# The first aggregation behind two gates begun early, two tiles turned by products, and 14 repeated products in a wait

## The chip, the cores and the metric

The kernel runs on one core of a Trainium2 chip. The metric is the device time of one execution in microseconds (us). TensorE does the matrix products (the trace calls it PE, and its weight loads PEld), VectorE is DVE, ScalarE is ACT, GpSimd is POOL, and SyncE (SP) issues most transfers.

## The reference

256 nodes with 768 features run through four blocks, each `x = x + block(relu(layernorm(x)))`, on a graph of 4352 edges:

```python
# block 0: two relational layers, each with a gate behind it
h = relu(rgcn(x, W_rel1, W_root1, b1)); h = gate(h, q, Wg, bg, Wq, bq)
h = relu(rgcn(h, W_rel2, W_root2, b2)); h = gate(h, q, Wg, bg, Wq, bq)
# rgcn: out = x @ root + bias + sum over relations r of mean over r's edges of (x @ W_r)[src]
# gate: attn = sigmoid(h @ Wg_h + q @ Wg_q + bg) for 64 queries of each of 8 graphs
#       qi = sum_l attn * q;  alpha = sigmoid(h @ Wq_h + qi @ Wq_q + bq)
#       h = alpha * tanh(qi) + (1 - alpha) * h
# block 1: three relational layers with four relations
# block 2: two graph attention layers (4 heads, 1 head), then an MLP 256 -> 256 -> 768
# block 3: two graph attention layers (8 heads of 96, 1 head of 768)
```

## The kernel before

The nodes lie in two tiles of 128 partitions, `t = 0, 1`; the 768 features are six chunks of 128 (`KC`). There are five relational layers, numbered 0 to 4: layers 0 and 1 with three relations, each followed by a gate, layers 2 to 4 with four relations. Every engine runs its own program in the order in which it is written, and semaphores tie the programs together. So what TensorE does next is fixed by hand, and a wait holds all that stands behind it.

In a layer (`layer_products`), TensorE first turns the second tile of H (`turn(1, e)`, six transposes of 128x128 into banks 6 and 7 of the PSUM tile `ps`), which VectorE copies to `h_t` (`keep_turned`, L1637, semaphore `turn_kept[1]`). The root's product on plain fp32 weights (`root`, `plain`, L957, behind a bias product, L951) is done for one tile after the other; each of its instructions is two passes in the trace. The relations go another way: `aggregate(layer, v)` (L1018) multiplies H by the count matrix of relation v (`A3` or `A4`), in three steps of two chunks (banks 4, 5 and 6), and for each chunk in four passes of 256 columns: the two node tiles, each as a high and a low part (`h_hi`, `h_lo`), summed in PSUM. That is 24 passes a relation. VectorE scales the sums (L1661), ScalarE and VectorE split them into `yt_hi` and `yt_lo`, and `product` (L987) multiplies them by the weights, which ScalarE (`w_hi`) and GpSimd (`w_lo`, L544) have split likewise. The weights come through four slots of `w_raw`; SyncE loads a slot when its last content has been used, and for the first relation's second and third slab behind a gate that content is the root's.

A gate takes 48 steps on VectorE, GpSimd, ScalarE and TensorE. It ends with the second tile: TensorE turns the gathered queries `qi_t` (L1372) into banks 4 and 5, ScalarE makes the tanh and the sigmoid, VectorE builds the new H (behind gate two, the new X, whose norm gives H). Meanwhile TensorE does `root(layer, 0, ...)` for the first tile of the next layer. Then, in the order of the program, it waits for the second tile's H, turns it, waits for both `h_lo` and for the copy of the turned tile, and begins the first aggregation.

The first tile's H is done earlier, within the gate's last steps; its turned form goes through bank 7 and is copied by ScalarE (`keep_half`, semaphores `half_kept` and `turn_kept[0]`).

Behind the MLP, TensorE turns the first tile of the normed X (L1537, six transposes, the second three behind a wait of their own, as the norm comes in two halves); ScalarE copies it (L864), and twelve passes of `logit_rows` (L1399) and the projections (L1414) follow.

Of the kernel before, what the change touches and what calls it, by code (L numbers as in the profile page):

```python
# [16 lines left out]
P = 128  # L17
N = 256
# [112 lines left out]
def build(nc, x, ei, qT, consts, brows, gbias, gavec, W, out):  # L131
    ctx = ExitStack()
    with ctx:
# [275 lines left out]
        def chunk_tile(bank, chunks):  # L409

            return ps[:, bank:bank + (chunks + 3) // 4, :].rearrange("p b n -> p (b n)")[:, 0:chunks * P].rearrange("p (k n) -> p k n", n=P)
# [535 lines left out]
        def _(pe):  # L947
# [11 lines left out]
            def turn(t, e):  # L959

                pe.wait_ge(h_ready[t], e + 1)
                for k in range(KC):
                    ins = pe.transpose(chunk_tile(4 + 2 * t, KC)[:, k, :], H[:, t, k * P:(k + 1) * P], ident[:])
                ins.then_inc(turned[t], 1)

            def root_bias(layer, bank):
# [39 lines left out]
            def aggregate(layer, v):  # L1006
# [3 lines left out]
                for j in range(3):  # L1010
# [9 lines left out]
                                n += 1  # L1020
                    ins.then_inc(sums_ready, 1)

            def product(layer, v, j, t, last):

                U = UNIT[layer] + v
                wait_lo(pe, U, j)
                pe.wait_ge(yt_lo_ready, BEFORE[layer] + 3 * (v - 1) + (j + 1))
                return three_terms(v % 2, j, t, pair(layer, t), last)

            def layer_products(layer, degrees=None):  # L1030

                e, R = INPUT[layer], RELATIONS[layer]
                if layer > 2:
                    root_part(layer, 0, 0)
                    turn(1, e)
                    root_part(layer, 0, 1)
                    root_part(layer, 0, 2)
                elif layer > 0:
                    root(layer, 0, 4, KC)
                    turn(1, e)  # L1040
                else:
                    turn(1, e)
                    root(layer, 0, 4, KC)
# [4 lines left out]
                if layer > 2:  # L1048
                    for j in range(3):
                        root_part(layer, 1, j)  # L1050
                for t in range(NT):
                    pe.wait_ge(h_lo_ready[t], layer + 1)
                if layer < 3:
                    pe.wait_ge(turn_kept[1], e + 1)
                if layer == 2:
                    pe.wait_ge(a4_ready, 1)
                aggregate(layer, 1)
                if layer < 3:
                    root(layer, 1, 4 if degrees is not None else 0, KC)
                aggregate(layer, 2)  # L1060
# [473 lines left out]
            for k in range(KC):  # L1534
                if k % 3 == 0:
                    pe.wait_ge(norm_h_ready, 3 + k // 3)
                ins = pe.transpose(chunk_tile(4, KC)[:, k, :], H[:, 0, k * P:(k + 1) * P], ident[:])  # L1537
            ins.then_inc(t_done, 1)
            pe.wait_ge(mlp_added, 3)
            logit_rows(2, 0)  # L1540
# [660 lines left out]
```

## Time and profile before

| | us |
|---|---|
| median of three timed runs | 845.45 |
| lowest, highest | 845.36, 847.61 |
| the profiled execution | 843.38 |
| its span, from first to last instruction | 841.6 |

The busy shares of the profiled execution are 93% for TensorE, 72% for VectorE, 58% for GpSimd and 49% for ScalarE. Times within the trace are counted from the span's start. Gate one ends and layer 1 begins at about 273 us, gate two ends and layer 2 begins at about 496 us, and the turn behind the MLP is at 771.5 us. A row of a timeline has the start, the time from the first start to the last end, the engine, the line, what is written from what, and the count; in brackets stands how long the engine was idle ahead of it and what released it. "PEclk" is the granted clock of TensorE as a share of 2.4 GHz.

### The profile page before, as it was taken

Reading aid. Unit: us, or ns where it says so; the run is one execution under the profiler, and the core shown is the slowest. Engines: PE = TensorE matmul, PEld = TensorE weight load, DVE = VectorE, ACT = ScalarE, POOL = GpSimd, SP = SyncE. Lnnn points to the kernel's source line nnn. Section 1 sums busy time; section 2 is a strip of 40 time slices with the busy share of each in tenths; the row PEclk is TensorE's granted clock in tenths of the full one; section 3 lists DMA queues with packets and bytes.
Section 4 is the critical chain, followed back from the end, with each engine's and each line's share of the span. In section 5 each row is a group of like instructions: output and inputs, shape, how many; then the busy total and the mean of one; then the engine's idle time right before and its main releaser. Section 6 shows DMA issues by size and latency. Waiting matters only on the chain.

```text
span 841.6 us, 10299 instructions
## 1 busy us (share of the span) xinstructions
PE 781.2 (93%) x4082; PEld 632.8 (75%) x4082; DVE 605.4 (72%) x665; ACT 411.8 (49%) x487; POOL 485.3 (58%) x211
## 2 busy tenths in 40 slices
PE   7999999999879999988988869999999999977998
PEld 4669976776556799667656548999999999755674
DVE  8965249999998623988999976555986495754442
ACT  6414367677663442776776623434535434142421
POOL 0626529999995461799999935841873397000000
PEclk9999999999999999999999989999999999999999
DMA  9046516344332553450444237564464463610001
GB/s 366 19 107 232 180 38 178 81 139 146 129 112 69 169 175 112 117 135 1 160 143 133 77 113 262 172 204 163 140 223 150 150 225 113 246 55 0 1 1 39
DMA packets 24410, 111.01 MB, mean 132 GB/s; under 512 B 3621, under 2 KB 6181, under 8 KB 23977
## 3 DMA queue, kind: packets, MB, share of 16 engines
q1 hardware_dynamic: 23240, 104.24, 38.1%
q10 hardware_dynamic: 1120, 6.10, 1.9%
q8 instruction: 33, 0.54, 0.3%
q14 instruction: 17, 0.13, 0.0%
HBM read 100.63 MB, written 0.79 MB: 121 GB/s over the span
## 4 chain that ended last, share of the span: by engine, by line
PE 60%; DVE 20%; POOL 14%; ACT 4%; issue 2%; DMA 0%; DVEq 0%; ACTq 0%
PE ps L987 27%; DVE prod L1778 11%; POOL prod L556 10%; PE ps L957 7%; PE ps L1018 6%; PE ps L1414 3%; DVE qi_t L1796 3%; POOL prod L559 3%; PE ps L1274 2%; PE ps L1095 2%; PE ps L1116 2%; PE ps L1227 2%; PE ps L1473 1%; PE ps L1399 1%; POOL w_lo L544 1%
## 5 line engine op out<-in xcount | busy, mean ns | idle before, releaser
L544 POOL TENSOR_TENSOR w_lo<-w_raw,w_hi 128x1536 fp32r<-128x1536 f32 x49 | 184.0, 3767 | 147.2 <-ACT w_hi L621 147.0
L556 POOL TENSOR_TENSOR prod<-prod 128x1024 f32<-128x1024 f32 x94 | 222.8, 2393 | 46.7 <-DVE prod L1778 46.4
L755 ACT ACTIVATE prod<-ps 128x1024 f32<-128x1024 f32 x192 | 187.3, 1023 | 74.0 <-PE ps L1227 61.6
L1778 DVE TENSOR_TENSOR prod<-prod,ps 128x2048 f32<-128x2048 f32 x96 | 217.7, 2280 | 6.3 <-ACT prod L755 4.7
L621 ACT ACTIVATE w_hi<-w_raw 128x1536 fp32r<-128x1536 f32 x60 | 88.9, 1487 | 123.5 <-PE ps L987 108.7
L1227 PE MATMUL ps<-sel_pair,h_and_q 128*128 128x512 f32 x384 | 129.1, 449 | 16.8 <-ACT prod L755 16.5
L987 PE MATMUL ps<-w_hi,yt_hi 128*128 128x384 f32 x480 | 122.9, 336 | 0.3 <-POOL w_lo L544 0.2
L987 PE MATMUL ps<-w_hi,yt_lo 128*128 128x384 f32 x480 | 121.9, 334 | 0.0
L987 PE MATMUL ps<-w_lo,yt_hi 128*128 128x384 f32 x480 | 121.8, 334 | 0.0
L957 PE MATMUL ps<-w_raw,h_t 128*128 128x384 f32 x312 | 106.8, 486 | 0.0
L1227 PEld LDWEIGHTS ps<-sel_pair,h_and_q 128*128 128x128 f32 x384 | 67.4, 191 | 52.1 <-ACT prod L755 31.8
L987 PEld LDWEIGHTS ps<-w_lo,yt_hi 128*128 128x128 f32 x480 | 86.8, 188 | 0.0
L987 PEld LDWEIGHTS ps<-w_hi,yt_lo 128*128 128x128 f32 x480 | 86.7, 188 | 0.0
L987 PEld LDWEIGHTS ps<-w_hi,yt_hi 128*128 128x128 f32 x480 | 85.4, 188 | 1.1 <-POOL w_lo L544 1.1
L957 PEld LDWEIGHTS ps<-w_raw,h_t 128*128 128x128 f32 x312 | 58.8, 189 | 33.9
L1661 DVE TENSOR_TENSOR ps<-ps,rinv 128x512 f32<-128x512 f32 x54 | 37.0, 695 | 61.3 <-PE ps L1018 60.7
L1274 PEld LDWEIGHTS ps<-prod,ident 128*128 128x128 f32 x464 | 57.3, 198 | 17.9 <-issue 9.7
L1274 PE MATMUL ps<-prod,ident 128*128 128x128 f32 x464 | 60.0, 285 | 10.9 <-POOL prod L556 10.9
L1018 PE MATMUL ps<-a,h_hi 128*128 128x256 f32 x216 | 56.1, 297 | 5.0 <-DVE h_t L1637 2.1
L1796 DVE TENSOR_REDUCE qi_t<-prod 128x32 f32<-128x512 f32 (+1 forms) x67 | 59.0, 885 | 2.3 <-POOL prod L559 2.0
L559 POOL TENSOR_TENSOR prod<-prod 128x512 f32<-128x512 f32 x45 | 58.2, 1293 | 3.5
L621 ACT ACTIVATE yt_hi<-ps 128x512 fp32r<-128x512 f32 (+1 forms) x58 | 35.0, 612 | 43.3 <-DVE ps L1661 42.8
(198 smaller groups left out, 1003.3 us busy)
## 6 DMA issues: line engine op xcount, KB each, us to landing
w_raw<-weights SPq DMA_DIRECT2D x105, 768.0 KB, 4.4
wa_in<-weights SPq DMA_DIRECT2D x6, 768.0 KB, 6.0
w_gat<-weights SPq DMA_DIRECT2D x6, 768.0 KB, 8.1
w_query<-weights SPq DMA_DIRECT2D x3, 768.0 KB, 11.9
h_and_q<-stage_hi SPq DMA_DIRECT2D x24, 96.0 KB, 2.1
h_and_q<-stage_lo SPq DMA_DIRECT2D x24, 96.0 KB, 2.2
a_vec<-gat_vectors ACTq DMA_DIRECT2D x1, 2048.0 KB, 9.6
q_t<-queries ACTq DMA_DIRECT2D x1, 1536.0 KB, 12.0
```

Of the source, the lines that this page charges most:

```text
L544: pool.tensor_tensor(Wl[:, j, :], raw_slab(U, 0, j), Wh[:, j, :], ALU.subtract).then_inc(w_lo_by_pool, 1)
L556: pool.tensor_tensor(v[:, :, 0:32], v[:, :, 0:32], v[:, :, 32:64], ALU.add).then_inc(folded_once, 1)
L559: pool.tensor_tensor(v[:, :, 0:16], v[:, :, 0:16], v[:, :, 16:32], ALU.add).then_inc(folded_twice, 1)
L621: return act.activation(o, i, ACT.Copy)
L755: act.activation(slot_view(s)[:, :, 32 * u:32 * u + 32], args.rearrange("p b (n l) -> p (b n) l", l=LH), ACT.Sigmoid).then_inc(sigmoid_rea ...
L957: return pe.matmul(ps[:, bank + h, 0:FH], left, raw_slab(U, c, k // 2)[:, o:o + FH], start=start, stop=stop)
L987: mm = pe.matmul(ps[:, bank + h, 0:FH], Y[:, s, k, t * P:(t + 1) * P], Wx[:, j, c0:c0 + FH], start=False, stop=(last and k == KC - 1 and n ...
L1018: ins = pe.matmul(ps[:, 4 + j, kk * N:(kk + 1) * N], Hx[:, t, k * P:(k + 1) * P], A[:, t, v - 1, :], start=(n == 0), stop=(n == 3))
L1227: mm = pe.matmul(ps[:, bank + h, :], HQ[:, b, u, f * P:(f + 1) * P], SEL[:, h * 512:(h + 1) * 512], start=True, stop=True)
L1274: mm = pe.matmul(o, ident[:], slot_view(s)[:, :, 4 * k:4 * k + 4], start=(k == 0), stop=(k == 7))
L1778: TT(slot_view(s), slot_view(s), ps[:, 6, o:o + L].unsqueeze(1).broadcast_to([P, NB, L]), ALU.mult).then_inc(products_ready, 1)
L1796: dve.tensor_reduce(qiT[:, f, b * NB:(b + 1) * NB], terms, AX.X, ALU.add).then_inc(qi_ready, 1)
```

## The change

At the start of layers 1 and 2 the first aggregation is taken apart. `first_aggregate(layer, 0)` does the first node tile's share of the first four chunks: for each of banks 4 and 5 one product with a row of zeros over all 512 columns, which starts the bank's sum, and four passes that add to it. `first_aggregate(layer, 1)` adds the second tile's share when its `h_lo` is there. `last_of_first_aggregate` does the last two chunks whole in bank 6, behind the copy of the turned tile. In layer 1 the first part stands behind the turn of the second tile, in layer 2 ahead of it.

In layer 2, 14 equal products (`keep_clock`, the shape of an aggregation pass, into bank 7, where nothing reads them) stand between the first part and the turn.

The second tile's turn in layer 2 and the first tile's turn behind the MLP are done by an ordinary fp32 product with the unit matrix in place of a transpose.

```diff
                 for k in range(KC):
-                    ins = pe.transpose(chunk_tile(4 + 2 * t, KC)[:, k, :], H[:, t, k * P:(k + 1) * P], ident[:])
+                    to, tile = chunk_tile(4 + 2 * t, KC)[:, k, :], H[:, t, k * P:(k + 1) * P]
+                    if t == 1 and e == INPUT[2]:
+                        ins = pe.matmul(to, tile, ident[:], start=True, stop=True)
+                    else:
+                        ins = pe.transpose(to, tile, ident[:])
                 ins.then_inc(turned[t], 1)
...
+            def first_aggregate(layer, t):
+
+                A = A3 if layer < 2 else A4
+                if t == 0:
+                    pe.wait_ge(tanh_ready, 4 * layer)
+                    if layer == 2:
+                        pe.wait_ge(a4_ready, 1)
+                pe.wait_ge(h_lo_ready[t], layer + 1)
+                for j in range(2):
+                    if t == 0:
+                        pe.wait_ge(yt_lo_ready, BEFORE[layer] - 2 + j)
+                        pe.matmul(ps[:, 4 + j, :], selb[0:1, 0, :], selb[0:1, 1, 0:1].broadcast_to([1, 2 * N]),
+                                  start=True, stop=False)
+                    for kk in range(2):
+                        k = 2 * j + kk
+                        for n, Hx in enumerate((Hh, Hl)):
+                            ins = pe.matmul(ps[:, 4 + j, kk * N:(kk + 1) * N], Hx[:, t, k * P:(k + 1) * P], A[:, t, 0, :],
+                                            start=False, stop=(t == 1 and kk == 1 and n == 1))
+                    if t == 1:
+                        ins.then_inc(sums_ready, 1)
+
+            def keep_clock(layer):
+
+                for n in range(14):
+                    pe.matmul(ps[:, 7, 0:N], Hh[:, 0, 0:P], A4[:, 0, 0, :], start=True, stop=True)
+
+            def last_of_first_aggregate(layer):
+
+                A = A3 if layer < 2 else A4
+                pe.wait_ge(turn_kept[1], INPUT[layer] + 1)
+                pe.wait_ge(yt_lo_ready, BEFORE[layer])
...
                     root(layer, 0, 4, KC)
+                    if layer == 2:
+                        first_aggregate(layer, 0)
+                        pe.wait_ge(half_kept, 2)
+                        pe.wait_ge(turn_kept[0], 5)
+                        keep_clock(layer)
                     turn(1, e)
+                    if layer == 1:
+                        first_aggregate(layer, 0)
...
-                for t in range(NT):
-                    pe.wait_ge(h_lo_ready[t], layer + 1)
-                if layer < 3:
-                    pe.wait_ge(turn_kept[1], e + 1)
-                if layer == 2:
-                    pe.wait_ge(a4_ready, 1)
-                aggregate(layer, 1)
+                if layer in (1, 2):
+                    first_aggregate(layer, 1)
+                    last_of_first_aggregate(layer)
+                else:
+                    for t in range(NT):
+                        pe.wait_ge(h_lo_ready[t], layer + 1)
+                    if layer == 0:
+                        pe.wait_ge(turn_kept[1], e + 1)
+                    aggregate(layer, 1)
...
                     pe.wait_ge(norm_h_ready, 3 + k // 3)
-                ins = pe.transpose(chunk_tile(4, KC)[:, k, :], H[:, 0, k * P:(k + 1) * P], ident[:])
+                ins = pe.matmul(chunk_tile(4, KC)[:, k, :], H[:, 0, k * P:(k + 1) * P], ident[:], start=True, stop=True)
```

TensorE's order behind gate one (layer 1). `sel_row` is the row of zeros, `a_64` the count matrix. Before, from the last root part of the first tile:

```order
L957 MATMUL ps<-w_raw,qi_t 128x384 x2
L957 MATMUL ps<-w_raw,h_t 128x384 x4
L963 MATMUL ps<-ident,h 128x128 x6
L1018 MATMUL ps<-a_64,h_hi 128x256
L1018 MATMUL ps<-a_64,h_lo 128x256
```

And now:

```order
L957 MATMUL ps<-w_raw,h_t 128x384 x4
L967 MATMUL ps<-ident,h 128x128 x6
L1038 MATMUL ps<-sel_row 128x512
L1043 MATMUL ps<-a_64,h_hi 128x256
L1043 MATMUL ps<-a_64,h_lo 128x256
...
L1038 MATMUL ps<-sel_row 128x512
```

The turn keeps its place; the first tile's share of the aggregation, with its two zero products, follows it, and the second tile's share comes behind that.

TensorE's order behind gate two (layer 2), with the semaphores that a row waits for. Before:

```order
L957 MATMUL ps<-w_raw,h_t 128x384 x3
L963 MATMUL ps<-ident,h 128x128 [waits h_ready1]
L963 MATMUL ps<-ident,h 128x128 x5
L1018 MATMUL ps<-a_100,h_hi 128x256 [waits a4_ready,turn_kept1,yt_lo_ready,h_lo_ready1,h_lo_ready0]
L1018 MATMUL ps<-a_100,h_lo 128x256
```

And now, from the last passes of the first tile's share on:

```order
L1043 MATMUL ps<-a_100,h_hi 128x256
L1043 MATMUL ps<-a_100,h_lo 128x256
L1051 MATMUL ps<-a_100,h_hi 128x256 [waits turn_kept0,half_kept]
L1051 MATMUL ps<-a_100,h_hi 128x256 x13
L965 MATMUL ps<-ident,h 128x128 [waits h_ready1]
L965 MATMUL ps<-ident,h 128x128 x5
L1043 MATMUL ps<-a_100,h_hi 128x256 [waits h_lo_ready1]
```

The first tile's share and the 14 repeated products now stand ahead of the wait for the second tile, and the wait for the turned tile's copy has moved from the first pass of the aggregation to its 17th.

## Rows read from the trace of the kernel before

**Rows 1.** The page: busy time of the engines, and the chain by engine.
```profile
PE 781.2 (93%) x4082; PEld 632.8 (75%) x4082; DVE 605.4 (72%) x665; ACT 411.8 (49%) x487; POOL 485.3 (58%) x211
...
PE 60%; DVE 20%; POOL 14%; ACT 4%; issue 2%; DMA 0%; DVEq 0%; ACTq 0%
```

**Rows 2.** Timeline, end of gate one: start, us, engine, line, count, [idle before].
```profile
273.30 0.87 PE L963 MATMUL ps<-ident,h 128*128 128x128 f32 x6 [0.32 <-DVE h L1825]
274.16 0.96 DVE L1632 TENSOR_TENSOR h_lo<-h,h_hi 128x768 fp32r<-128x768 f32 x1 [0.92 <-ACT h_hi L621]
...
275.03 0.95 DVE L1637 COPY h_t<-ps 128x768 f32<-128x768 f32 x1
...
276.24 0.36 PE L1018 MATMUL ps<-a,h_hi 128*128 128x256 f32 x1 [2.07 <-DVE h_t L1637]
...
279.16 0.51 PE L951 MATMUL ps<-bias,sel_row 128*128 128x384 f32 x2
```

**Rows 3.** Timeline, end of gate two.
```profile
496.24 0.87 PE L963 MATMUL ps<-ident,h 128*128 128x128 f32 x6 [3.81 <-ACT h L640]
...
497.11 0.96 DVE L1632 TENSOR_TENSOR h_lo<-h,h_hi 128x768 fp32r<-128x768 f32 x1 [1.98 <-ACT h_hi L621]
497.98 0.95 DVE L1637 COPY h_t<-ps 128x768 f32<-128x768 f32 x1
...
499.14 0.55 PE L1018 MATMUL ps<-a,h_hi 128*128 128x256 f32 x1 [2.03 <-issue]
...
504.27 0.51 PE L951 MATMUL ps<-bias,sel_row 128*128 128x384 f32 x2
```

**Rows 4.** Stretches: PE, PEld, DVE, ACT, POOL busy (count), PEclk, DMA share, GB/s.
```profile
272.90:276.20 3.30, 0.95 (x7) 0.64 (x6) 2.38 (x4) 2.26 (x2) 0.00 (x0) 1.00 0.30 123
...
492.50:495.90 3.40, 0.00 (x0) 0.00 (x0) 1.82 (x6) 0.74 (x1) 0.55 (x1) 1.00 0.26 107
495.90:499.10 3.20, 0.87 (x6) 0.64 (x6) 1.88 (x3) 2.51 (x3) 0.58 (x1) 0.71 0.57 184
499.10:504.20 5.10, 5.06 (x24) 5.09 (x25) 4.38 (x5) 1.13 (x2) 2.87 (x1) 0.51 0.53 196
...
773.80:777.20 3.40, 3.40 (x14) 2.53 (x13) 0.28 (x1) 1.00 (x2) 0.00 (x0) 0.51 0.00 0
```

**Rows 5.** Timeline, two folds of a gate's step on TensorE (16 fp32 passes).
```profile
257.08 1.95 PE L1274 MATMUL ps<-prod,ident 128*128 128x128 f32 x16
...
377.69 3.65 PE L1274 MATMUL ps<-prod,ident 128*128 128x128 f32 x16 [0.55 <-POOL prod L556]
```

**Rows 6.** Timeline of several engines in layer 2's first relation.
```profile
501.59 0.70 DVE L1661 TENSOR_TENSOR ps<-ps,rinv 128x512 f32<-128x512 f32 x1
...
511.70 1.49 ACT L621 ACTIVATE w_hi<-w_raw 128x1536 fp32r<-128x1536 f32 x1 [5.89 <-DMA w_raw<-weights]
...
513.26 6.98 POOL L544 TENSOR_TENSOR w_lo<-w_raw,w_hi 128x1536 fp32r<-128x1536 f32 x2 [11.29 <-ACT w_hi L621]
...
515.23 0.52 PE L987 MATMUL ps<-w_hi,yt_hi 128*128 128x384 f32 x2
```

**Rows 7.** Waits from 500 to 730: who waited for whom, us, times, longest.
```profile
PE ps L1018 <- DVE yt_lo L1665: 0.9, 2, 0.4
...
PE ps L987 <- POOL w_lo L544: 0.2, 1, 0.2
```

**Rows 8.** Timeline of TensorE, the turn behind the MLP and passes after it.
```profile
771.50 1.15 PE L1537 MATMUL ps<-ident,h 128*128 128x128 f32 x6 [0.66 <-ACT h L919]
773.59 2.62 PE L1399 MATMUL ps<-h_t,w_logit 128*40 128x128 f32 x12 [0.95 <-issue]
776.13 2.04 PE L1414 MATMUL ps<-w_gat,h_t 128*128 128x384 f32 x4
...
779.10 1.45 PE L1414 MATMUL ps<-w_gat,h_t 128*128 128x384 f32 x4
780.49 1.50 PE L1399 MATMUL ps<-h_t,w_logit 128*40 128x128 f32 x12
```

More of the change, by code:

```diff
@@ L1021, in aggregate @@
                     ins.then_inc(sums_ready, 1)
+            def first_aggregate(layer, t):
[24 more added lines that the diff above has]
+                pe.wait_ge(yt_lo_ready, BEFORE[layer])
+                for kk in range(2):
+                    k = 4 + kk
+                    n = 0
+                    for t in range(NT):
+                        for Hx in (Hh, Hl):
+                            ins = pe.matmul(ps[:, 6, kk * N:(kk + 1) * N], Hx[:, t, k * P:(k + 1) * P], A[:, t, 0, :],
+                                            start=(n == 0), stop=(n == 3))
+                            n += 1
+                ins.then_inc(sums_ready, 1)
             def product(layer, v, j, t, last):
@@ L1050, in layer_products @@
                         root_part(layer, 1, j)
-                for t in range(NT):
-                    pe.wait_ge(h_lo_ready[t], layer + 1)
-                if layer < 3:
-                    pe.wait_ge(turn_kept[1], e + 1)
-                if layer == 2:
-                    pe.wait_ge(a4_ready, 1)
-                aggregate(layer, 1)
+                if layer in (1, 2):
+                    first_aggregate(layer, 1)
+                    last_of_first_aggregate(layer)
+                else:
+                    for t in range(NT):
+                        pe.wait_ge(h_lo_ready[t], layer + 1)
+                    if layer == 0:
+                        pe.wait_ge(turn_kept[1], e + 1)
+                    aggregate(layer, 1)
                 if layer < 3:
```

## The prediction

> **What bounds the kernel now.** I read the page first, for the engines' totals and the chain that ended last [rows 1]. TensorE is busy 93% of the span and carries 60% of the chain; the reader is to see that it is the bound of the aggregation layers, and that the rest of the chain belongs to the two gates, where VectorE and GpSimd set the pace. Then the order of time around the two gates' ends and around the last turned tile, because the diff touches only these places. I call them **place one** (end of gate one, layer 1), **place two** (end of gate two, layer 2) and **place three** (the turn ahead of the last graph attention pair). Last, the granted clock by stretches, since an aggregation pass that takes 0.12 us at place one takes 0.21 us at place two.
>
> Place one [rows 2]: the six transposes of the second tile run from 273.30, VectorE then makes h_lo (to 275.12) and copies the turned tile (to 275.98), and the 24 aggregation passes start at 276.24; the root's bias product follows at 279.16. So TensorE waits 2.07 us for the copy, and does 24 passes of 0.12 us behind it.
>
> Place two [rows 3]: TensorE waits 3.81 us for the second tile, from 492.43, where it has done the root's part; the transposes start at 496.24, h_lo is there at 498.07, the copy at 498.93, the passes start at 499.14, and the bias product only at 504.27: 5.13 us for the same 24 passes that took 2.92 us at place one.
>
> The clock [rows 4]: full (2.4 GHz) from 492.50 to 495.90, when TensorE did nothing, 0.71 on average from 495.90 to 499.10, and 0.51 (1.2 GHz but for the last moment) from 499.10 to 504.20. It fell after the wait, and stayed low for nearly the whole first aggregation. From 773.80 to 777.20 the mean is 0.51 again, behind the turn at place three.
>
> **The change, part by part.** A duration "per pass" is a start-to-start distance.
>
> *Place one, the split aggregation.* Eight of the 24 passes (the first tile's share of four of the six chunks) and two new products that write zeros (one row, 512 columns, one for each of two banks) now follow the turn at once. They need h_lo of the first tile and the gate's tanh, both there before the turn starts. Eight passes are 8 x 0.12 = 0.96 us. The trace has no such zero product; by columns it is two passes of 256, 0.24 us, which I take; below it can't be under one pass (0.12), and above I allow 0.51, the length of a whole pair of weight passes on the bias [rows 2]. 0.96 + 0.48, begun at about 274.1 (the turn's last start, and 0.1 for the waits), ends at 275.55. The second tile's h_lo lands at 275.12 and with the 0.26 us that TensorE needs after VectorE's end [rows 2] would let it go at 275.4, so it goes on at 275.6: 8 passes to 276.6, and 8 more of the last two chunks, which need the copy (275.98 + 0.26 = 276.24, past). End 277.6 where it was 279.16: **1.6 us**, bounds 1.0 and 1.9.
>
> *Place two, the same with the repeated products.* From 492.43 the two zero products and eight passes take 1.44 us, to 493.9; all of it lies in the 3.81 us wait. The 14 repeated products (the same shape as an aggregation pass, 0.12 us each) take 1.7 us more, to 495.6, before the tile is there at 496.2, so they cost nothing while the second tile comes this late; with an earlier tile they would cost up to 1.7. The two waits ahead of them are for copies on ScalarE that were done inside the gate. The turn is now 12 product passes of 0.12 us (so the fold, the same fp32 product with the unit matrix: 16 in 1.95 us [rows 5]) instead of six transposes in 0.87: 11 x 0.12 + 0.28 for the last = 1.6 us, to 497.85. The copy waits for it, but VectorE is on h_lo until 498.07 [rows 3], so the 0.7 us is hidden; without that cover it would be 0.7 late. The second tile's passes start at 498.07 + 0.2 = 498.3 and end at 499.25 at the full clock; the last eight need the copy (498.93 + 0.2 = 499.15) and end at 500.3. The bias product comes at 500.3 where it was 504.27: **3.95 us**, of which 1.0 is the earlier start, 0.9 the eight passes done in the wait and 2.1 the clock. That the clock stays full I take from this: the idle time between 492.4 and 499.1 shrinks from 5.85 us in two pieces to about 0.6 and 0.5 us with products on either side, and at place one the clock stayed at 1.00 from 272.90 to 276.20 [rows 4], a stretch in which TensorE was busy for 0.95 us of 3.30.
>
> *Does it pass on?* VectorE's own chain at place two (copy, a fill, the reciprocal, the first scaling at 501.59) doesn't move, but its results are first used by the products at 515.23, now 511.3: it has some 7 us [rows 6]. The two later slabs of weights of the first relation are what could take the gain back: ScalarE splits the second at 511.70, having waited for its transfer, and GpSimd makes both low parts from 513.26 to 520.24 [rows 6]. That transfer is issued when the root's first two chunks have been used, so it moves with the root, by the same 3.95. From 500 to 730 TensorE waits only 0.9 us for yt_lo and 0.2 us for w_lo [rows 7]; I let all of both gains through.
>
> *Place three.* The six transposes become 12 product passes [rows 8]; the second half's three, which the chain runs through, take 5 x 0.12 + 0.28 = 0.88 us instead of 0.55: **0.35 us later**. What it may give back is the clock: the 12 passes at 773.59 take 2.62 us and the same 12 at 780.49 take 1.50, the four at 776.13 take 2.04 and the same four at 779.10 take 1.45 [rows 8]. That is 1.12 + 0.59 = 1.7 us, and from there on TensorE has no gap [rows 8]. If the clock holds, the place gives 1.7 - 0.35 = **1.35 us**; if not, it costs 0.35.
>
> The Trainium skill, "TensorE: Matmul & The Clock Gate", Part 4, says that a turn in transpose mode does not count as busy for the clock gate in the way a matmul does. By it, products in place of transposes add 1.6 us of counted work and place three holds. The trace does not bear it out clearly: with nothing but six transposes from 272.97 to 276.24 the clock stayed full [rows 2, 4]. If transposes do count, the products add only 0.7 us, and place three is likelier to lose its 0.35.
>
> **The sum.** 1.6 + 3.95 + 1.35 = 6.9 us. It is made on the profiled execution, 843.38 us with a span of 841.6, which is 2.07 us under the median of the timed runs (845.45). Taken from the median it gives 838.55; I say 838.6. Stretches of half clock need not fall at the same places in every execution: in this one there is also one inside gate two, where a fold that takes 1.95 us took 3.65 [rows 5]. One such stretch more or less is about 2 us, and the range has it on both sides.
>
> **Rivals.**
> *A, the clock is low at place two in spite of the repeated products.* For it: 14 products may be too little, and the trace has none like them in a wait. Against: the idle time is down to a fifth. The 16 passes behind the turn then take 3.4 us instead of 1.9 and the root runs at half until about 504.1, another 1.1 us: place two gives 1.4, the sum is 4.35, **841.1**.
> *B, place three doesn't hold.* For it: there TensorE still idles 0.66 us ahead of the turn and 0.95 behind it, and nothing is put into these gaps. 1.6 + 3.95 - 0.35 = 5.2, **840.2**.
> *C, the gain of place two is taken back by something that doesn't move,* the second slab's transfer or the split behind it, since the chain of weights starts with a DMA that lands when it likes. If it and what follows kept their times, nothing of the 3.95 would be left by layer 3: 1.6 + 1.35 = 2.95, **842.5**; with B as well 844.2. Against it: the order of the issues, above.
> *D, slower than before.* The half clock falls onto the root's 24 passes at place two and the products behind: with few transposes and short waits left the chip might grant 1.2 GHz for longer. Each 1 us of TensorE work at half clock costs 1 us, so it takes 6.9 us of work, 13.8 us of time, to use up the gain; three such stretches on end cost 10.2 us of time for 5.1 of work, four cost 6.8. The longest in this trace is about 7 us, from 497 to 504 [rows 4]. Five (8.5 us lost) would give **847**, six 848.8.
>
> **How the numbers follow.** Forecast 0.60, A 0.11, B 0.17, C 0.09, D 0.03. About 0.3%, 2.5 us, is what a measurement of this kernel can tell from no change: faster means under 842.9, slower over 848.0. The forecast, A, B and half of C are faster, with some lost to the spread of the runs (before: 845.36 to 847.61): 0.88. The rest of C and most of D are the same: 0.10. Slower 0.02. The range must hold 0.8: from 836.3 (the forecast, with one stretch of half clock less than before) to 842.2 (A and B with 1 us on top, C left out).
>
> **What would show it.** Right: TensorE's first aggregation pass at place two stands ahead of the turn; the granted clock between the turn and the root is 1.00; the bias product follows the turn's start by about 4.1 us at place two (was 8.0) and 4.3 at place one (was 5.9); the logit passes behind place three take 1.5 us. Wrong: 0.21 us per pass behind the turn at place two (A), 2.6 us for the logit passes (B), a wait of TensorE for w_lo in layer 2's first relation (C). The prediction falls if the zero products take much more than 0.24 us, if the turn by products makes VectorE's copy late, or if the clock's stretches in the gates move by more than one.

## The result and the profile after

The changed kernel takes 840.17 us (median of 7 executions, 835.23 to 841.04) against 845.43 for the kernel before (842.13 to 847.61): ratio 0.9941, 95% interval 0.992 to 0.9962. It is faster, by 5.3 us. The forecast was 838.6 with a range from 836.3 to 842.2. Run again beside other kernels, the change took 838.62 us (835.87 to 839.32) against 845.18: ratio 0.991 (0.9886 to 0.9934). So it gains 5.3 to 6.6 us in the medians, where 6.9 was forecast.

Its profiled execution (841.04 us, span 839.2) is the longest of its seven, and the one of before (843.38) lies 2 us under its median: the two traces differ by only 2.4 us. The page of after, the engines' busy time and the shares of its chain of waits:

```profile
PE 788.2 (94%) x4112; PEld 637.7 (76%) x4112; DVE 604.9 (72%) x665; ACT 411.9 (49%) x487; POOL 484.8 (58%) x211
PE 63%; DVE 19%; POOL 13%; ACT 3%; issue 1%; DMA 0%; DVEq 0%; ACTq 0%
```

TensorE is still the engine that bounds, as in [rows 1]. Read by segments, the two traces show what the order of the work gives and what the clock takes elsewhere.

**Place one.** Timeline of TensorE and VectorE behind gate one (start, us, engine, line, [idle before]; L967 is the turn, L1038 a zero product, L1043 the two shares of the first chunks, L951 the root's bias):

```profile
273.70 0.87 PE L967 MATMUL ps<-ident,h 128*128 128x128 f32 x6 [0.32 <-DVE h L1879]
274.50 0.48 PE L1038 MATMUL ps<-sel_row 1*128 1x512 f32 x1
274.56 0.96 DVE L1686 TENSOR_TENSOR h_lo<-h,h_hi 128x768 fp32r<-128x768 f32 x1 [0.92 <-ACT h_hi L621]
274.91 0.38 PE L1043 MATMUL ps<-a,h_hi 128*128 128x256 f32 x1
275.14 0.28 PE L1043 MATMUL ps<-a,h_lo 128*128 128x256 f32 x1
...
275.58 0.48 PE L1038 MATMUL ps<-sel_row 1*128 1x512 f32 x1
...
275.99 0.38 PE L1043 MATMUL ps<-a,h_hi 128*128 128x256 f32 x1
...
278.46 0.51 PE L951 MATMUL ps<-bias,sel_row 128*128 128x384 f32 x2
```

From the turn's start to the bias product it is 4.76 us, where [rows 2] give 5.86: **1.10 us** gained. The wait of 2.07 us for the copy is gone. A zero product holds the next pass for 0.41 us (274.50 to 274.91).

**Place two.** L1051 are the repeated products, L965 the turn by products:

```profile
494.21 1.83 PE L1051 MATMUL ps<-a,h_hi 128*128 128x256 f32 x14
...
496.03 1.60 PE L965 MATMUL ps<-ident,h 128*128 128x128 f32 x12
...
496.88 0.96 DVE L1686 TENSOR_TENSOR h_lo<-h,h_hi 128x768 fp32r<-128x768 f32 x1 [1.97 <-ACT h_hi L621]
497.76 0.95 DVE L1691 COPY h_t<-ps 128x768 f32<-128x768 f32 x1
497.90 0.39 PE L1043 MATMUL ps<-a,h_hi 128*128 128x256 f32 x1 [0.27 <-DVE h_lo L1686]
...
499.92 0.51 PE L951 MATMUL ps<-bias,sel_row 128*128 128x384 f32 x2
```

The bias product follows the turn's start by 3.89 us instead of 8.03 [rows 3]: **4.14 us**. The passes are 0.12 us apart again, the wait of 3.81 us is gone and the one of 2.03 us is down to 0.27 ahead of the second share, and VectorE's copy starts 0.88 us behind h_lo's start, as before (0.87), so the longer turn is hidden. The repeated products end at 496.04, just when the tile comes: the 0.5 us that the forecast saw between them went into the zero products.

**Place three.** L1591 is the turn by products, L1453 the logit passes, L1468 the projection:

```profile
770.32 1.60 PE L1591 MATMUL ps<-ident,h 128*128 128x128 f32 x12 [0.65 <-ACT h L919]
772.87 1.48 PE L1453 MATMUL ps<-h_t,w_logit 128*40 128x128 f32 x12 [0.95 <-issue]
774.28 1.56 PE L1468 MATMUL ps<-w_gat,h_t 128*128 128x384 f32 x4
```

From the turn's start to the logits it is 2.55 us instead of 2.09 (0.46 lost), from the logits to the span's end 66.35 instead of 67.99 (1.64 gained); the 12 logit passes take 1.48 us where [rows 8] have 2.62. **1.2 us** in all.

**The rest.** That is 6.45 us of gain, and the spans differ by 2.4. The difference lies where the diff changes nothing: 0.4 us ahead of place one, 0.5 in gate two, and 3.2 between place two's bias and place three's turn (270.40 us against 267.23 before). The stretches of the change (PE, PEld, DVE, ACT, POOL busy with counts, PEclk, DMA share, GB/s):

```profile
402.00:406.00 4.00, 3.91 (x18) 3.84 (x19) 4.00 (x4) 0.73 (x1) 3.92 (x3) 0.57 0.00 0
...
496.00:500.00 4.00, 3.73 (x30) 3.52 (x30) 2.97 (x4) 2.22 (x2) 1.70 (x1) 1.00 0.54 215
743.70:750.50 6.80, 6.75 (x30) 5.28 (x28) 3.05 (x11) 0.65 (x2) 0.00 (x0) 0.50 0.00 0
757.40:760.80 3.40, 2.85 (x9) 1.89 (x8) 1.61 (x6) 0.38 (x1) 0.00 (x0) 0.50 0.00 0
```

The clock is full at place two, where [rows 4] have 0.51, and halved for 10.2 us in the first two attention layers, where the profile of before had none. Half of 10.2 would be 5.1 us if every pass were bound by the clock; it costs 3.2 here. Whether the change brought that half clock there, or each execution draws it anew, is the first question for the experiments.

### The profile page after: what moved, and what is told of

Its sections match the earlier page's. It is cut to its first block, busy times and chain, and to the rows that moved or that the text cites. A ratio compares the mean times of both kernels' runs of the same rounds, so it can differ in the third digit from the quotient of the medians.

```text
span 839.2 us, 10361 instructions
## 1 busy us (share of the span) xinstructions
PE 788.2 (94%) x4112; PEld 637.7 (76%) x4112; DVE 604.9 (72%) x665; ACT 411.9 (49%) x487; POOL 484.8 (58%) x211
## 4 chain that ended last, share of the span: by engine, by line
PE 63%; DVE 19%; POOL 13%; ACT 3%; issue 1%; DMA 0%; DVEq 0%; ACTq 0%
PE ps L991 28%; DVE prod L1832 10%; POOL prod L556 10%; PE ps L957 7%; PE ps L1022 5%; PE ps L1468 3%; DVE qi_t L1850 3%; POOL prod L559 3%; PE ps L1328 2%; PE ps L1149 2%; PE ps L1170 2%; PE ps L1281 2%; PE ps L1527 2%; PE ps L1453 1%; PE ps L1150 1%
## 5 line engine op out<-in xcount | busy, mean ns | idle before, releaser
L991 PE MATMUL ps<-w_hi,yt_hi 128*128 128x384 f32 x480 | 122.9, 336 | 0.0
L991 PE MATMUL ps<-w_hi,yt_lo 128*128 128x384 f32 x480 | 121.8, 334 | 0.0
L991 PE MATMUL ps<-w_lo,yt_hi 128*128 128x384 f32 x480 | 121.8, 334 | 0.0
L991 PEld LDWEIGHTS ps<-w_lo,yt_hi 128*128 128x128 f32 x480 | 86.8, 188 | 0.0
L991 PEld LDWEIGHTS ps<-w_hi,yt_lo 128*128 128x128 f32 x480 | 86.7, 188 | 0.0
L991 PEld LDWEIGHTS ps<-w_hi,yt_hi 128*128 128x128 f32 x480 | 85.4, 188 | 0.8 <-POOL w_lo L544 0.8
L1702 DVE TENSOR_TENSOR w_lo<-w_raw,w_hi 128x1536 fp32r<-128x1536 f32 x11 | 20.0, 1815 | 44.5 <-ACT w_hi L621 44.5
```

The lines of the kernel that those rows point to most:

```text
L991: mm = pe.matmul(ps[:, bank + h, 0:FH], Y[:, s, k, t * P:(t + 1) * P], Wx[:, j, c0:c0 + FH], start=False, stop=(last and k == KC - 1 and n ...
```

## The experiments

"Turn to bias" is from the start of the second tile's turn to the root's bias product, in each run's own profile. The clock's column has the lowest and the highest mean granted clock among a kernel's executions (4 to 12 of the changed kernels, 17 or 23 of before beside them).

| kernel | median us | ratio (95%) | clock | turn to bias, one / two | 12 logit passes | half clock, 735 to 765 |
|---|---|---|---|---|---|---|
| before | 845.4 | 1 | 0.984 to 0.994 | 5.86 / 8.03 | 2.62 | none |
| the change | 840.17 | 0.9941 (0.992 to 0.9962) | 0.987 to 0.996 | 4.76 / 3.89 | 1.48 | 10.2 |
| the change again | 838.62 | 0.991 (0.9886 to 0.9934) | 0.993 to 0.996 | 4.75 / 3.89 | 1.47 | 10.2 |
| split only | 842.16 | 0.9963 (0.994 to 0.9986) | 0.984 to 0.990 | 4.76 / 5.40 | 2.48 | 6.8 |
| no repeats | 841.70 | 0.9952 (0.9926 to 0.9978) | 0.985 to 0.996 | 4.76 / 3.88 | 1.48 | 10.2 |
| transposes | 838.86 | 0.9917 (0.9885 to 0.995) | 0.988 to 0.994 | 4.75 / 3.89 | 1.47 | 3.4 |
| no zeros | 838.99 | 0.9923 (0.9893 to 0.9954) | 0.989 to 0.992 | 3.87 / 3.88 | 1.48 | 6.8 |
| no zeros, transposes | 838.90 | 0.9913 (0.9887 to 0.9939) | 0.988 to 0.996 | 3.87 / 3.90 | 1.48 | 3.4 |
| repeats alone | 844.31 | 0.998 (0.9957 to 1.0002) | 0.986 to 0.996 | 7.39 / 5.83 | 2.65 | 6.8 |
| fills alone | 843.14 | 0.9969 (0.9946 to 0.9992) | 0.990 to 0.996 | 7.38 / 8.12 | 1.48 | none |
| filled | 834.97 | 0.9876 (0.9852 to 0.99) | 0.996 to 0.998 | 3.87 / 3.89 | 1.48 | none |
| filled, no repeats | 836.90 | 0.9889 (0.9855 to 0.9923) | 0.992 to 0.994 | 3.87 / 5.46 | 1.48 | none |
| filled, products | 834.83 | 0.9881 (0.9842 to 0.992) | 0.996 to 1.0 | 3.87 / 3.89 | 1.48 | none |
| filled, zeros | 834.83 | 0.9867 (0.983 to 0.9904) | 0.995 to 1.0 | 4.76 / 3.89 | 1.48 | none |

### The split aggregations alone

The 14 repeated products are left out, and both turns are transposes:

```diff
-                        pe.wait_ge(half_kept, 2)
-                        pe.wait_ge(turn_kept[0], 5)
-                        keep_clock(layer)
...
-                        ins = pe.matmul(to, tile, ident[:], start=True, stop=True)
+                    ins = pe.transpose(to, tile, ident[:])
```

> The change with its split aggregations alone: no repeated products at place two, transposes at both turned tiles. My theory (the split gives 1.1 us at place one and 2.0 us at place two in every execution; the clock is a separate gain that needs the repeated products or the product turns): the aggregation passes behind the turn at place two still start ahead of it, the clock falls there in this profile or in a good part of the executions (0.21 us a pass), the 12 logit passes behind place three take up to 2.6 us. Total 3 to 4 us below the kernel before, ratio 0.995 to 0.9965. Rival (the split itself keeps the clock, because its passes sit in the wait): full clock at place two, ratio 0.994, the same as the change.

842.16 us, ratio 0.9963: inside what my theory gave. The rival's 0.994 is the lower end of the interval, so it is the profile, where the clock is not full at place two, that speaks against it. TensorE's timeline at place two (L964 the turn, L1040 the second share):

```profile
493.88 0.87 PE L964 MATMUL ps<-ident,h 128*128 128x128 f32 x6 [1.66 <-ACT h L640]
495.75 0.52 PE L1040 MATMUL ps<-a,h_hi 128*128 128x256 f32 x1 [1.00 <-DVE h_lo L1680]
496.08 0.42 PE L1040 MATMUL ps<-a,h_lo 128*128 128x256 f32 x1
496.29 0.42 PE L1040 MATMUL ps<-a,h_hi 128*128 128x256 f32 x1
...
499.28 0.52 PE L951 MATMUL ps<-bias,sel_row 128*128 128x384 f32 x2
```

The passes are 0.21 us apart: the clock fell behind 1.66 and 1.00 us of idle time with six transposes between. The split's gain at place two is 8.03 - 5.40 = 2.6 us with the clock low in both; part of that is that fewer passes stand in the low stretch (3.4 us of half clock here, 6.8 before).

### Without the repeated products, and with transposes

> The change without the 14 repeated products. TensorE then idles about 1.8 us ahead of the turn at place two. My theory: with the first part of the aggregation ahead and 12 product passes behind, the idle time no longer is long enough in most executions, full clock in the profile, ratio 0.994 to 0.995. Rival (the 14 products are what holds the clock): 0.21 us a pass behind the turn at place two, root's bias product about 6 us behind the turn's start instead of 3.9, ratio 0.996 to 0.997.

841.70 us, ratio 0.9952. The one profile has a full clock at place two (3.88 us), as my theory said, so the split and the product turn were enough in that execution. But its 12 executions go from 837.53 to 845.85, and the interval holds both readings; this run doesn't settle what the 14 products do.

The other half of the same question, the change with its repeats but with transposes:

> The change with transposes again at both turned tiles; the 14 repeated products stay. If transposes count for the clock as little as no work, the idle time at place two is 1.9 us from the last repeated product to the first pass of the second tile, and place three is as before: low clock behind it (12 logit passes in 2.6 us) in the executions in which it fell before. Expected total 0.5 to 1.5 us above the change, ratio 0.9945 to 0.996. Rival (transposes count like products): full clock at place three, and 0.46 us less there than with products; ratio 0.9935 to 0.994.

838.86 us, ratio 0.9917, and place three had a full clock in this profile, with 2.09 us from turn to logits. That is the rival's side, and lower than either reading gave; but the "split only" profile has transposes at the same place with a low clock behind (2.48 us). With transposes the 12 logit passes were at half clock in three of five profiles without fills (before, split only, repeats alone: 2.62, 2.48, 2.65), with products in none of four. That speaks for the products, and is too little to show it.

### Without the zero products

```diff
-                        pe.matmul(ps[:, 4 + j, :], selb[0:1, 0, :], selb[0:1, 1, 0:1].broadcast_to([1, 2 * N]),
-                                  start=True, stop=False)
...
-                                            start=False, stop=(t == 1 and kk == 1 and n == 1))
+                                            start=(t == 0 and kk == 0 and n == 0), stop=(t == 1 and kk == 1 and n == 1))
```

> The change without its four zero products: the first pass into each bank starts the bank's sum, and the first pass into its other half just writes. In the trace of the change a zero product costs 0.41 us to the next pass and that pass another 0.11 us, two of them 1.04 us at place one, of which the wait for the second tile's h_lo hides 0.3. Theory: place one is 0.75 us shorter (bias product 4.0 us behind the turn's start, was 4.76), place two unchanged (they lie in the wait there), and the rest as in the change; ratio 0.993. Rival (the passes are held by h_lo and by the copy of the turned tile anyway): under 0.3 us at place one, ratio 0.994.

Place one is 0.89 us shorter in the profile (3.87 against 4.76; 0.75 was expected). The total is 838.99, with an interval that holds the change's too, so it doesn't show the difference. TensorE at place one:

```profile
273.30 0.88 PE L967 MATMUL ps<-ident,h 128*128 128x128 f32 x6 [0.32 <-DVE h L1877]
273.93 0.36 PE L1041 MATMUL ps<-a,h_hi 128*128 128x256 f32 x1
274.13 0.28 PE L1041 MATMUL ps<-a,h_lo 128*128 128x256 f32 x1
...
277.17 0.51 PE L951 MATMUL ps<-bias,sel_row 128*128 128x384 f32 x2
```

The eight passes of the first share take 1.0 us, and in the change the same eight with two zero products 2.07 (274.50 to 276.57). So nothing rests on the zero products: with `start` on the pass that begins the bank's first half alone, the sum in its other half comes out too.

### The change again, and no zeros with transposes

> The change itself once more, so that its profile and its executions stand beside others of the same hour. Theory (where the clock is low is drawn anew in each execution; the order of the work gives 1.10 us at place one and about 4.1 at place two every time): turn to bias 4.76 and 3.89 us again, 2.55 us and 1.48 us at place three, but the half-clock stretches of 740 to 760 us are elsewhere, shorter or gone in this profile. Rival (the change itself moves half clock into the first attention layer): at least 6.8 us of half clock between 735 and 765 us again. Ratio 0.994 by both.

The segments of the three places are the same to 0.01 us. The half clock in the attention layers is not elsewhere: 6.8 us from 741.5 and 3.4 us from 755.2, and counted from the start of place three's turn that is within 0.5 us of the first profile. So far the rival stands. What differs is the gates: the first profile has half clock at 252, 402 and 433 us, this one has none there, and from place one's bias product to place two's turn it takes 215.98 us (first profile 217.57, before 217.08).

> Split aggregations without zero products, with the 14 repeated products, transposes at both turned tiles. If the gains add as the segments say: place one 3.87 us (turn to bias), place two 3.89, place three 2.09 us from turn to logits, clock at place three low in some executions (2.5 us for the 12 passes) and full in others (1.48). Ratio 0.9915 to 0.993. Rival (the product turns matter for the clock more than they cost): ratio 0.994.

838.90 us, ratio 0.9913, just below the expected 0.9915 and clear of the rival's 0.994 by the interval. The segments are as expected, 1.35 us less than in the change (0.89 at place one, 0.46 at place three), but the medians don't show it: the change in the same comparison has 838.62. Of half clock in the attention layers there are 3.4 us.

### Repeated products alone, on the kernel before

```diff
+                    if layer == 2:
...
+                        for n in range(26):
+                            pe.matmul(ps[:, 7, 0:N], Hh[:, 0, 0:P], A4[:, 0, 0, :], start=True, stop=True)
                     turn(1, e)
```

There are 26 of them where the change has 14, and left out of the diff are the waits for what they read and for the bank that they write.

> The kernel before with nothing but 26 repeated products (3.1 us) in the wait of 3.8 us ahead of the turn at place two; aggregation whole and behind the copy, transposes everywhere. Theory (at place two the clock's share is 2.1 us and the products alone give it back): full clock behind the turn, turn to bias 5.9 us as at place one before, ratio 0.997 to 0.9985. Rival (the wait for the copy, 2.0 us behind six transposes, brings the clock down all the same): 8.0 us from turn to bias, ratio 1.0.

844.31 us, ratio 0.998 (0.9957 to 1.0002), as expected and not distinct from no change. Turn to bias at place two is 5.83 us in its profile, 2.2 less than before: there the repeated products alone give back the clock, with transposes, and with the wait of 2 us behind the turn still in place. The mean clocks agree: they make 16.9 us of half clock in the mean of its 12 executions, and 20.7 in the 17 of before beside them. The profile answers two more questions. Its stretches:

```profile
272.00:276.50 4.50, 2.11 (x15) 1.48 (x14) 3.55 (x5) 2.33 (x2) 0.63 (x1) 1.00 0.31 128
276.50:280.00 3.50, 3.50 (x20) 3.50 (x19) 2.57 (x4) 1.15 (x2) 2.85 (x1) 0.52 0.00 0
497.00:503.00 6.00, 3.67 (x29) 3.46 (x30) 4.65 (x5) 2.47 (x3) 3.42 (x1) 1.00 0.75 262
747.70:754.50 6.80, 6.75 (x28) 4.96 (x28) 2.99 (x11) 0.65 (x2) 0.00 (x0) 0.50 0.00 0
```

First, the unsplit order of place one loses the clock too (276.50 to 280.00), and turn to bias is 7.39 us there instead of 5.86. It did so in two of the three profiles of the old order (this and "fills alone"), and in none of the eleven of the split order. Second, the old order has 6.8 us of half clock in the attention layers as well (from 747.70). So the change isn't needed for it. That it makes it more frequent is not excluded: without fills, all seven profiles of the split order have half clock there, and of the two of the old order one.

### The filled kernel

Based on "no zeros, transposes", with 15 products that nothing reads in four waits of the attention layers:

```diff
+            def fill(bank, count):
+
+                for n in range(count):
+                    pe.matmul(ps[:, bank, :].rearrange("p (a b) -> p a b", a=4), selb[:, 0, :], selb[:, 0:4, :], start=True, stop=True)
...
+            fill(5, 4)
+            fill(4, 5)
+            fill(4, 3)
+            fill(6, 3)
```

The four calls stand ahead of the first attention layer's weighted sums, ahead of the second layer's turned weights, behind them, and behind place three's turn.

> The kernel of the no-zeros-with-transposes run, and 15 more products that nothing reads, 512 columns each, in waits of TensorE of 0.9 to 1.3 us in the first two attention layers (4, 5 and 3) and behind the turn at place three (3). Theory (the half clock of 740 to 760 us and behind place three follows low activity there): no half clock from 735 to 780 us in the profile, turn to logits at place three unchanged at 2.09, mean granted clock over the executions 0.992 or more, ratio 0.990 to 0.992. Rival (the stretch of 65-column passes, in which weight loads bound TensorE, brings the clock down by itself): the same stretch of 3.4 or 6.8 us from about 743, ratio as without the extra products, 0.992.

834.97 us, ratio 0.9876 (0.9852 to 0.99), 3.9 us under the same kernel without the fills and the lowest so far; its four executions lie from 834.48 to 835.30. TensorE's timeline (L1433 the fills, L1527 the weighted sums):

```profile
738.36 1.18 PE L1433 MATMUL ps<-sel_row 128*128 128x512 f32 x4
739.48 3.79 PE L1527 MATMUL ps<-h_aug,attn 128*128 128x65 f32 x32
...
748.35 1.49 PE L1433 MATMUL ps<-sel_row 128*128 128x512 f32 x5
...
766.40 1.48 PE L1453 MATMUL ps<-h_t,w_logit 128*40 128x128 f32 x12 [0.25 <-issue]
```

Two stretches of the same profile, with the columns as above:

```profile
738.00:750.00 12.00, 11.20 (x70) 8.27 (x68) 6.65 (x17) 2.68 (x9) 0.00 (x0) 1.00 0.00 1
750.00:760.00 10.00, 8.12 (x33) 5.25 (x34) 4.56 (x11) 1.82 (x5) 0.00 (x0) 1.00 0.00 0
```

The 32 passes of 65 columns take 3.79 us, where the change's profile has 5.44 for the same 32, and the clock is full throughout; the rival, that these passes bring it down by themselves, has fallen. (In the profile of before the same 32 passes took 3.76 us behind the same wait and without fills, so they don't always lose the clock.) From place two's bias to place three's turn it is 266.83 us (270.40 in the change, 267.23 before). Of the nine profiles without fills eight have half clock between 735 and 765 us, of the five with fills none.

### The filled kernel as a base

With its narrow spread it tells differences that the others can't.

> The filled kernel (its four executions lie within 0.8 us, so it is a sharper base) without the 14 repeated products at place two; transposes at the turn. Theory (without them TensorE idles 2.3 us ahead of the turn and about 1 us behind it, and the clock falls there in a part of the executions): some executions as the filled kernel (835.0), others up to 2.3 us above it, granted clock 0.002 to 0.004 lower on average, median ratio 0.988 to 0.991. Rival (the split alone is enough, the repeated products do nothing): all executions at 834.5 to 835.5, ratio 0.9876.

Six executions from 836.08 to 837.30: 1.9 us above in the median, and in all of them, not in a part only as my theory had it. The rival has fallen: the repeated products are worth 1.9 us when the turn is by transposes. At place two (L964 the turn, L1038 the second share):

```profile
492.80 1.11 PE L964 MATMUL ps<-ident,h 128*128 128x128 f32 x6 [2.86 <-ACT h L640]
494.68 0.58 PE L1038 MATMUL ps<-a,h_hi 128*128 128x256 f32 x1 [0.76 <-DVE h_lo L1687]
495.06 0.41 PE L1038 MATMUL ps<-a,h_lo 128*128 128x256 f32 x1
```

> The filled kernel with the change's product turns at both turned tiles in place of transposes. Theory (the products cost 0.46 us on the path at place three, nothing at place two because VectorE is still on h_lo, and the clock holds either way once the waits are filled): 0.4 to 0.5 us above the filled kernel, 835.4; turn to logits 2.55 us, turn to bias at place two 3.89. Rival (the clock still needs the products, transposes don't count): at or below 835.0 and a higher mean granted clock.

834.83 us in the median, but four executions at 834.17 to 834.86 and two at 839.04 and 839.42. The cost at place three is there (2.55 us, 2.09 with transposes) and isn't seen in the total; what the products give back isn't shown either. Its profile is one of the two long ones, and shows something else (below).

> The filled kernel with the change's four zero products back. Theory (each stalls TensorE by 0.41 us and the pass behind it by 0.11 us, at place one 0.9 us of it is on the path, at place two none): turn to bias at place one 4.76 us instead of 3.87, total 0.9 us above the filled kernel, 835.9, ratio 0.9887. Rival (a later wait, for the copy or the weights, takes the 0.9 us up): 835.0.

834.83 us, where 835.9 was expected. Turn to bias at place one is 4.76 us, 0.89 more than in the filled kernel, as my theory said, but the total doesn't show it. In the profiles, the filled kernel reached place one at 273.72 us, with half clock in gate one from 252.3, and this kernel at 273.09, with full clock all along; its executions have a mean clock of 1.0 in five of six, the filled kernel's 0.996 to 0.998. Whether that stretch is what makes up for the 0.9 us is not shown: the six profiles with half clock in gate one reach place one at 273.03 to 273.72 us, the eight without at 272.51 to 273.44. Why this kernel's executions are spared it I don't know. The rival's own reason, a later wait, isn't seen either: from place one's bias on the two profiles run alike to within 0.3 us.

> The kernel before with nothing but the filled kernel's 15 products in waits of the attention layers. Theory (half clock in the first attention layers and behind place three is drawn in the kernel before too, and costs it 1 to 3 us in most executions; places one and two stay as they are): no half clock from 735 to 780 us, from place three's logits to the end 66.3 us instead of 68.0, half clock at place two, turn to bias there about 7 to 8 us; ratio 0.9955 to 0.998. Rival (the fills only help the changed kernel, whose shifted work brought the half clock into the attention layers): ratio 0.998 to 1.0, the gain of place three's clock alone.

843.14 us, ratio 0.9969 (0.9946 to 0.9992), as my theory said: the fills help the old order too, by 1.6 us in the median. The interval reaches into the rival's 0.998. From place three's logits to the end it is 66.44 us (67.99 before). Places one and two have the low clock of the old order (7.38 and 8.12).

## Why the prediction was right

**Place one** gave 1.10 us, 1.6 was forecast. The term that was mis-sized is the zero product: 0.24 us by columns, 0.52 measured (0.41 to the next pass, 0.11 more for that pass), just past the upper bound of 0.51 that I had allowed. I had priced it by its columns alone, with no row of a one-row product to go by. Without the zero products place one gives 1.99.

What the forecast left out is the clock at place one. In the profile of before it was full there, and I took it so for all executions. In two other profiles of the old order it fell and cost 1.5 us (7.39 and 7.38 against 5.86); the split removes the wait that brings it down. So the mean gain of the split at place one is likely above 1.10; three profiles of the old order are few.

**Place two** gave 4.14 us, 3.95 was forecast, and its parts were right: the turn by products is hidden behind h_lo, the clock stays full, and the gain passes through layers 2 to 4. The runs give the parts as well: between profiles with a full clock the split is worth 5.83 - 3.89 = 1.94 us (1.9 was forecast), and the clock in the old order 8.03 - 5.83 = 2.20 (2.1). For the 14 repeated products the forecast's reason was the shorter idle time. The filled kernel without them agrees (1.9 us more), and in "repeats alone" 26 such products do it with nothing else changed (5.83 against 8.03). Both have transposes at the turn; whether the change, with its product turn, needs the 14 is not shown, since "no repeats" kept the clock in its profile. Rival A fell, and so did rival C: between place two and the attention layers TensorE waited for no w_lo in the change's profile.

**Place three** gave 1.2 us, 1.35 was forecast: the clock held (rival B fell in all five profiles with product turns), and the turn cost 0.46 us instead of 0.35. I had counted only the second half's three chunks; the first three take 0.7 us as products and now run into the second half's. That the products are why the clock held is not shown, since it also held behind transposes in two of five profiles without fills; part of this may be luck.

**The total** came out 1.6 us short of the forecast in the first comparison (840.17 against 838.6) and on it in the second (838.62). The sum of the segments is 6.45 us, 0.45 short, so the exact hit is luck. What doesn't follow from the segments is the half clock elsewhere, about which the forecast said only that one stretch more or less costs about 2 us. It is larger than that: twice the missing share of the mean clock, times the span, is the time at half clock, and in the second comparison that is 20.7 us in the mean of 17 executions of before (0.984 to 0.990) and 9.8 us in six of the change (0.993 to 0.996), in the first 16.8 us in seven of the change. The two first profiles have 17.1 (before) and 20.5 (the change), the other way round. Rival D, half clock that lasts, did not come, though its mechanism exists: half clock in the attention layers took 3.2 us of this profile's gain. The range was narrower than its own working: with A and B together the sum is 2.65 us, 842.8, which lies outside its upper end of 842.2.

One segment works for the change and is in nobody's account. From place one's bias product to place two's turn, where the diff changes nothing, the three profiles of the old order take 217.1 or 217.2 us, with half clock from about 378 or 379; of the eleven of the split order nine take 215.9 or 216.0, and none has half clock there (the other two take 216.9 and 217.6). No run shows why it stays away, and the 1.1 us may belong to the gain of most executions.

## What to carry to other kernels

A wait of TensorE can cost twice: its own length, and the clock behind it; so fill waits first with work that is due anyway (a partial sum of the tile that is ready), then with products that nothing reads, and put these also into short waits around passes of few columns. A pair of profiles can mislead when the clock is low in other stretches in each: compare segments between fixed points, and mean clocks over many executions, before a total is believed. Price a new kind of instruction with a wide bound above, even when it has few columns.

## What the runs showed of the hardware

**The zero product stalls TensorE.** With one row of weights and 512 columns it held the next pass for 0.41 us, where the fills, 128x512 columns, follow each other by 0.25 to 0.27 us (four in 1.18 and five in 1.49 us, with a mean record of 0.42). The zero product also reads one value over and over; whether the single row or that reading makes it slow, no run separates.

**The clock falls at few places, and at each in a part of the executions.** The change's two profiles are of one program: both have half clock in the attention layers, from 743.7 and 757.4 us and from 741.5 and 755.2, but only the first has it in the gates (from 252, 402 and 433). Over all 14 profiles half clock begins at 251 or 252 us in six and at 448 or 449 in five; at place one the old order kept the full clock in one profile and lost it in two. The Trainium skill, "TensorE: Matmul & The Clock Gate", Part 4, says that a transpose does not count as busy in the way a matmul does. The runs lean that way and don't settle it: place three was at half clock behind transposes in three of five unfilled profiles and never behind products, but the clock also held at place two with transposes behind repeated products, in five profiles ("transposes", "no zeros, transposes", "repeats alone", "filled" and "filled, zeros").

**A transfer that lands late turns into TensorE time.** The profile of "filled, products" is 4.4 us longer in span than that of "filled, zeros" (837.6 and 833.2). In layer 3's last relation, VectorE waits for the attention weights' transfer (L1941 here), which took 8.5 us from issue to landing where the same one in "filled, zeros" took 6.0, and all that it does for layer 4 is queued behind that. VectorE's timeline of "filled, products":

```profile
623.10 3.87 DVE L1941 TENSOR_TENSOR wa_tmp<-wa_in,a_vec 128x1536 f32<-128x1536 f32 x1 [4.50 <-DMA wa_in<-weights]
...
633.92 1.76 DVE L1709 TENSOR_TENSOR w_lo<-w_raw,w_hi 128x1536 fp32r<-128x1536 f32 x1 [0.18 <-DVE w_logit L1945]
```

TensorE in the same profile, with the projection that takes w_lo (L991):

```profile
635.74 0.68 PE L991 MATMUL ps<-w_hi,yt_hi 128*128 128x384 f32 x2 [2.96 <-DVE w_lo L1709]
636.22 0.84 PE L991 MATMUL ps<-w_lo,yt_hi 128*128 128x384 f32 x2
```

VectorE's timeline of "filled, zeros" at the same place (L1940, L1708):

```profile
621.20 1.76 DVE L1940 TENSOR_TENSOR wa_tmp<-wa_in,a_vec 128x1536 f32<-128x1536 f32 x1 [1.97 <-DMA wa_in<-weights]
...
630.79 2.15 DVE L1708 TENSOR_TENSOR w_lo<-w_raw,w_hi 128x1536 fp32r<-128x1536 f32 x1 [1.06 <-ACT w_hi L621]
```

The wait is 4.50 us instead of 1.97, w_lo starts 3.1 us later, TensorE stands for 2.96 us, and the clock falls behind that (passes at 0.32 us instead of 0.17; half clock from 636.15 to 639.57). The two executions at 839 us of this kernel, and those of the kernel before at 847 to 851 us, may all be this; only the one profile shows it. An order in which VectorE makes that w_lo ahead of the attention weights wasn't tried.
